# A radial network computed per edge block, dense products two node groups later, and own rows summed last, in a three-stage graph kernel

## The reference, cut to what matters

```python
# stage A and B: two preln GCN layers, N = 6250 nodes, D = 512, E = 100000 edges sorted by dst
h = layer_norm(x, g0, be0)                        # x is itself relu(layer_norm(input)) here
h = relu(gcn_conv(h, row, col, W0, b0) + h @ lw0.T + lb0); x_final = h
h = layer_norm(h, g1, be1)
h = relu(gcn_conv(h, row, col, W1, b1) + h @ lw1.T + lb1)
out = (x_final + h) @ pw.T + pb                   # row/col hold the edges and a loop per node
# stage C: equivariant messages; the radial network needs only the edges' 8 features
h = edge_feats                                    # (100000, 8)
for W in (W_mlp1, W_mlp2, W_mlp3):                # hidden 64
    h = SILU_2MOM * silu(h @ W / sqrt(W.shape[0]))
tpw = h @ W_mlp4 / sqrt(64)                       # weights of the messages, summed by receiver
```

## Time and profile before

| | us |
|---|---|
| median of 3 runs | 5891.26 |
| lowest and highest | 5843.2, 5891.44 |
| the profiled execution, its own time | 5896.5 |
| its span, first to last instruction | 5894.7 |
| layer 0, from its first own-row matmul to its last group's yb | 532.5 to 1809 |
| layer 1, the same | 1842 to 3392 |

### The profile page before, as it was taken

One profiled execution on the slowest core, in us unless ns is written; L12 is line 12 of the kernel. 1 busy time (PEld: TensorE's weight loads), 2 busy tenths in 40 slices (PEclk: granted clock), 3 DMA queues, 4 the chain that ended last, 5 costly groups with the idle time before them and its releaser, 6 DMA issues.

```text
span 5894.7 us, 104811 instructions
## 1 busy us (share of the span) xinstructions
PE 4878.7 (83%) x17136; PEld 2263.9 (38%) x17137; DVE 2857.1 (48%) x8231; ACT 2308.6 (39%) x6178; POOL 2737.7 (46%) x3492
## 2 busy tenths in 40 slices
PE   6897566778886567787777889999999999999988
PEld 5443122333332123333333334444444444444444
DVE  7542122334442112222222257777777777777776
ACT  0441000111110012233333466666666666666665
POOL 0334766666664766654433234444443333333332
PEclk9998678889997678899899999999999999999999
DMA  2233666677775666776666534444444334333333
GB/s 81 96 107 125 185 187 205 210 219 232 230 233 153 183 201 207 227 234 200 198 186 182 176 115 120 117 116 116 119 118 119 115 115 118 115 116 115 117 115 97
DMA packets 433673, 916.80 MB, mean 156 GB/s; under 512 B 63094, under 2 KB 170870, under 8 KB 433511
## 3 DMA queue, kind: packets, MB, share of 16 engines
q0 software_dynamic: 195840, 641.89, 37.5%
q1 hardware_dynamic: 237798, 274.56, 14.2%
HBM read 787.79 MB, written 128.41 MB: 155 GB/s over the span
## 4 chain that ended last, share of the span: by engine, by line
PE 31%; issue 21%; DVE 10%; DMA 8%; ACT 8%; DVEq 7%; ACTq 5%; POOL 5%; POOLq 2%; another core or an unknown queue 2%; SPq 1%
PE bank L1220 7%; DMA ring<-tab_d,idx 6%; POOL ring L559 4%; PE bank L1269 3%; PE bank L1350 3%; PE bank L1191 3%; PE bank L1193 3%; DVEq L1078 3%; ACT hB L756 3%; ACT dense_w L767 3%; ACTq L753 2%; PE bank L1253 2%; DVE hA L1086 2%; DMA tw<-tab_d 2%
## 5 line engine op out<-in xcount | busy, mean ns | idle before, releaser
L559 POOL DMA_INDIRECT ring<-tab_d,idx x1568 | 1541.6, 983 | 909.4 <-issue 549.1
L1350 PE MATMUL bank<-dense_w,oh 128*128 128x512 f32 x3520 | 1619.8, 603 | 66.9 <-DVE dense_w L1095 66.4
L1220 PE MATMUL bank<-ring,ohp 128*128 x3904 | 1084.6, 439 | 422.2 <-POOLq L569 330.9
L525 POOL DMA_INDIRECT ring<-up_d,idx x880 | 880.4, 1000 | 498.4 <-POOL idx L521 348.6
L767 ACT ACTIVATE dense_w<-hA,hC 128x128 f32<-128x128 f32 x2640 | 820.2, 389 | 654.8 <-DVE hA L1086 600.1
L1350 PEld LDWEIGHTS bank<-dense_w,oh 128*128 128x128 f32 x3520 | 633.1, 190 | 858.8 <-issue 668.1
L1220 PEld LDWEIGHTS bank<-ring,ohp 128*128 x3904 | 421.1, 108 | 1065.7 <-issue 763.6
L983 DVE TENSOR_TENSOR ohp<-iota_w,dst_f 128x512 f32 x392 | 266.1, 691 | 703.5 <-PE bank L1220 513.6
L521 POOL COPY idx<-src_i 128x2 int32 x440 | 81.2, 185 | 1045.2 <-DVE dense_w L1095 964.2
L1340 PE MATMUL bank<-w,hC 64*128 64x256 f32 x3520 | 501.9, 403 | 31.4 <-issue 22.9
L1072 DVE SCALAR_TENSOR_TENSOR hA<-ring,hC,hB 128x128 f32<-128x128 f32 x880 | 270.4, 348 | 490.3 <-ACT hB L756 428.3
(11 more groups left out here) (180 smaller groups left out, 4877.2 us busy)
## 6 DMA issues: line engine op xcount, KB each, us to landing
hC<-hid_d SPq DMA_DIRECT2D x440, 64.0 KB
tab_d<-tout SPq DMA_DIRECT2D x98, 256.0 KB, 2.7
tw<-tab_d SPq DMA_DIRECT2D x98, 256.0 KB
hlw<-hl_d SPq DMA_DIRECT2D x98, 256.0 KB
ring<-tab_d,idx POOLq DMA_INDIRECT x1568
hid_d<-hC SPq DMA_DIRECT2D x98, 256.0 KB
hl_d<-agg SPq DMA_DIRECT2D x74, 256.0 KB, 3.0
ring<-up_d,idx POOLq DMA_INDIRECT x880
```

Source lines behind the costliest of these rows:

```text
L525: g_.indirect_dma_start(ring_v[:, b, k, :], None, table, bass.IndirectOffsetOnAxis(idx_t[:, b, k:k + 1], 0)).then_inc(S["got"][b], 16)
L559: g_.indirect_dma_start(ring_h[:, b, k, :], None, table, bass.IndirectOffsetOnAxis(idx_b[:, b, k:k + 1], 0)).then_inc(S["got"][b], 16)
L1220: ins = pe.matmul(bank[0][:, :], ohp_b[:, bass.ds(at, 1), k, :].rearrange("p b n -> p (b n)"), ring_b[:, bass.ds(slot, 1), k, h, :].rearra ...
L1350: ins = pe.matmul(bank[h][:, :], oh[:, b, k, :], msg[:, b, k, h, :], start=False, stop=False, skip_group_check=True)
```

## The change

- **Radial per block.** In layer 1, PE and ACT take a step of the radial network after each edge block's visit, one piece per step, in the first 94 blocks: PE layer3(n), layer2(n+1), layer1(n+2), ACT act3(n), act2(n+1), act1(n+2), store_hid(n), load_ef(n+3). The first pieces' steps run ahead of the layer, the last three pieces are finished after it. ACT, not SP, now issues the feature loads (in layer 1, and the first two ahead of layer 0) and the stores of hid. One bank for each layer (4, 5, 6).
- **Later dense work.** Layer 0's turn, copy_at and dense run with delay 2 instead of 1, high, low and the stores with 3; turn now stands ahead of edge_sum. In layer 1 turn_xs, copy_xT and project have delay 2, residual, std, relu_h and store_x1 3, turn_h, copy_hT, up, up_out and store_up 4; both transposes stand ahead of edge_sum. up has bank 7 to itself.
- **Own rows last.** edge_sum starts bank 0 with the first visited block (group 0: an empty matmul) and waits for tw only after the group's last visit; the two own-row matmuls end the sum. load_self waits for sum_done.
- **Gathers.** Copy of the next indices and row 2 come before the wait for the block before and "arrived".

```diff
@@ -388,7 +387,7 @@
         S = G[L]
         def load_self(w, S=S, L=L):
-            after(sp, S["self_used"], w)
+            after(sp, S["sum_done"], w)
             sp.dma_start(tw[:, :], rows(tab_d[L], w)).then_inc(S["self_in"], 16)
         def load_hl(w, S=S, L=L):
@@ -426,32 +425,18 @@
             sp.wait_ge(S["up_ready"], w + 1)
             sp.dma_start(rows(up_d, w), uo[:, :]).then_inc(S["up_stored"], 16)
...
         if L == 0:
-            peeled(sp, [(0, load_self), (0, load_hl), (1, store_r), (2, store_tab), (2, store_hl)])
+            peeled(sp, [(0, load_self), (0, load_hl), (1, store_r), (3, store_tab), (3, store_hl)])
             sp.wait_ge(S["r_stored"], 16 * NW)
             sp.wait_ge(S["tab_stored"], 16 * NW)
             sp.wait_ge(S["hl_stored"], 16 * NW)
         else:
-            peeled(sp, [(0, load_ef), (0, load_self), (3, store_up), (0, load_hl), (4, store_hid), (0, load_r0),
-                        (1, load_x), (2, store_x1)])
+            peeled(sp, [(0, load_self), (0, load_hl), (0, load_r0), (2, load_x), (3, store_x1), (4, store_up)])
             sp.wait_ge(S["x1_stored"], 16 * NW)
             sp.wait_ge(S["up_stored"], 16 * NW)
-    sp.wait_ge(hid_out[0], 16 * (NG // 8))
-    sp.wait_ge(hid_out[1], 16 * (NG // 8))
+    sp.wait_ge(hid_out, 16 * (NG // 4))
     c = sp.alloc_register("sp_tp_count")
     sp.reg_mov(c, 1)
@@ -564,11 +549,11 @@
                     g_.reg_add(d, d, 1)
                     row(0)
                     row(1)
+                    g_.tensor_copy(idx_b[:, (b + 1) % NK, :], src_i[:, bass.ds(ahead, BT)]).then_inc(S["idx_ready"], 1)
+                    row(2)
                     with g_.If(n > LAG):
                         g_.wait_ge(S["got"][(b - LAG) % NK], landed)
                         g_.nop().then_inc(S["arrived"], 1)
-                    g_.tensor_copy(idx_b[:, (b + 1) % NK, :], src_i[:, bass.ds(ahead, BT)]).then_inc(S["idx_ready"], 1)
-                    row(2)
                     row(3)
                     g_.reg_add(c, c, 1)
                 pick(g_, g_.snap(n % NK), 0, NK, gather)
@@ -702,42 +687,89 @@
         def up_out(w, S=S):
             ac.wait_ge(S["up_done"], w + 1)
             after(ac, S["up_stored"], w, 16)
-            ac.copy(uo[:, :], bank[3][:, :]).then_inc(S["up_ready"], 1)
...
+            ac.copy(uo[:, :], bank[7][:, :]).then_inc(S["up_ready"], 1)
+        def act1(i):
+            ac.wait_ge(m1, i + 1)
+            if not isinstance(i, int) or i > 0:
+                ac.wait_ge(m2, i)
+            ac.activation(hA[:, 0, :], bank[4][:, :], ACT.Silu).then_inc(a1, 1)
+        def act2(i):
+            ac.wait_ge(m2, i + 1)
+            if not isinstance(i, int) or i > 0:
+                ac.wait_ge(m3, i)
+            ac.activation(hB[:, 0, :], bank[5][:, :], ACT.Silu).then_inc(a2, 1)
+        def act3(i):
+            ac.wait_ge(m3, i + 1)
+            to = hC[:, i % 2, :] if isinstance(i, int) else hC[:, bass.ds(i % 2, 1), :].rearrange("p b n -> p (b n)")
+            ac.activation(to, bank[6][:, :], ACT.Silu).then_inc(a3, 1)
+        def load_ef(i):
+            if not isinstance(i, int) or i > 1:
+                ac.wait_ge(ef_in, i * 16)
+                ac.wait_ge(m1, i - 1)
+            to = ef[:, i % 2, :] if isinstance(i, int) else ef[:, bass.ds(i % 2, 1), :].rearrange("p b n -> p (b n)")
+            ac.dma_start(to, a["ef_t"][:, bass.ds(i * D, D)]).then_inc(ef_in, 16)
+        def store_hid(i):
+            ac.wait_ge(a3, i + 1)
+            if not isinstance(i, int) or i > 0:
+                ac.wait_ge(hid_out, i * 16)
+            of = hC[:, i % 2, :] if isinstance(i, int) else hC[:, bass.ds(i % 2, 1), :].rearrange("p b n -> p (b n)")
+            ac.dma_start(hid_d[bass.ds(i * 4, 4), :, :].rearrange("g p e -> p g e"),
+                         of.rearrange("p (g e) -> p g e", g=4)).then_inc(hid_out, 16)
+        if L == 1:
+            c = ac.alloc_register("act_radial_count")
+            ac.reg_mov(c, 1)
+            def radial(w, c=c):
+                lo, hi = block_range(ac, w)
+                with ac.Fori(lo, hi) as g:
+                    n = ac.snap(c)
+                    with ac.If(n < NG // 4 - 3):
+                        act3(n)
+                        act2(n + 1)
+                        act1(n + 2)
+                        store_hid(n)
+                        load_ef(n + 3)
+                    ac.reg_add(c, c, 1)
         if L == 0:
-            peeled(ac, [(1, relu_r), (2, high), (1, std), (1, scaled), (1, copy_at)])
+            load_ef(0)
+            load_ef(1)
+            peeled(ac, [(1, relu_r), (3, high), (2, copy_at), (1, std), (1, scaled)])
         else:
-            peeled(ac, [(1, act1), (1, relu_r), (2, std), (2, relu_h), (2, act2), (1, copy_xT), (3, act3),
-                        (2, copy_hT), (2, up_out), (4, lambda w: None)])
+            act1(0)
+            load_ef(2)
+            act2(0)
+            act1(1)
+            load_ef(3)
+            act3(0)
+            act2(1)
+            act1(2)
+            store_hid(0)
+            peeled(ac, [(1, relu_r), (2, copy_xT), (4, copy_hT), (0, radial), (3, std), (3, relu_h), (4, up_out)])
+            last = NG // 4 - 1
+            act3(last - 2)
+            act2(last - 1)
+            act1(last)
+            store_hid(last - 2)
+            act3(last - 1)
+            act2(last)
+            store_hid(last - 1)
+            act3(last)
+            store_hid(last)
     c = ac.alloc_register("act_tp_count")
     ac.reg_mov(c, 1)
-    for b in range(2):
-        ac.wait_ge(hid_out[b], 16 * (NG // 8))
+    ac.wait_ge(hid_out, 16 * (NG // 4))
     ac.nop().then_inc(M["w13"], 1)
     ac.nop().then_inc(M["p2"], 1)
     lo_r, hi_r = ac.alloc_register("act_tp_lo"), ac.alloc_register("act_tp_hi")
@@ -1046,9 +1078,9 @@
             scale(0).then_inc(S["scale"], 1)
         if L == 0:
-            peeled(ve, [(1, layer_out), (0, onehots), (2, low), (1, second_norm)])
+            peeled(ve, [(1, layer_out), (0, onehots), (3, low), (1, second_norm)])
         else:
-            peeled(ve, [(1, layer_out), (0, onehots), (1, project_in), (2, residual)])
+            peeled(ve, [(1, layer_out), (0, onehots), (1, project_in), (3, residual)])
     c = ve.alloc_register("dve_tp_count")
@@ -1206,21 +1238,36 @@
         pe.reg_mov(v_r, 1)
         pe.nop().then_inc(S["used"], NV)
-        def edge_sum(w, S=S, c=c, v_r=v_r):
+        def layer1(i):
+            pe.wait_ge(ef_in, (max(i, 1) + 1) * 16 if isinstance(i, int) else i * 16 + 16)
+            if not isinstance(i, int) or i > 0:
+                pe.wait_ge(a1, i)
+            at = ef[:, i % 2, :] if isinstance(i, int) else ef[:, bass.ds(i % 2, 1), :].rearrange("p b n -> p (b n)")
+            pe.matmul(bank[4][:, :], w1[:, :], at, start=True, stop=True).then_inc(m1, 1)
+        def layer2(i):
+            pe.wait_ge(a1, i + 1)
+            if not isinstance(i, int) or i > 0:
+                pe.wait_ge(a2, i)
+            pe.matmul(bank[5][:, :], w2[:, :], hA[:, 0, :], start=True, stop=True).then_inc(m2, 1)
+        def layer3(i):
+            pe.wait_ge(a2, i + 1)
+            if not isinstance(i, int) or i > 0:
+                pe.wait_ge(a3, i)
+            pe.matmul(bank[6][:, :], w3[:, :], hB[:, 0, :], start=True, stop=True).then_inc(m3, 1)
+        def edge_sum(w, S=S, L=L, c=c, v_r=v_r):
             lo, hi = block_range(pe, w)
             after(pe, S["y_read"], w)
-            pe.wait_ge(S["self_in"], (w + 1) * 16)
-            pe.matmul(bank[0][:, :], ident_h[:, :], tw[:, 0:D], start=True, stop=False, skip_group_check=True)
-            pe.matmul(bank[0][:, :], ident_h[:, :], tw[:, D:], start=False, stop=False,
-                      skip_group_check=True).then_inc(S["self_used"], 1)
-            def visit(slot, at):
+            def visit(slot, at, first):
                 for k in range(BT):
                     for h in range(2):
                         ins = pe.matmul(bank[0][:, :],
                                         ohp_b[:, bass.ds(at, 1), k, :].rearrange("p b n -> p (b n)"),
                                         ring_b[:, bass.ds(slot, 1), k, h, :].rearrange("p b n -> p (b n)"),
-                                        start=False, stop=False, skip_group_check=True)
+                                        start=(first and k == 0 and h == 0), stop=False, skip_group_check=True)
                 ins.then_inc(S["used"], 1)
                 pe.reg_add(v_r, v_r, 1)
@@ -1228,15 +1275,25 @@
                 v, n = pe.snap(v_r), pe.snap(c)
                 slot, at = pe.snap((n - 1) % NK), pe.snap(v % NV)
                 pe.wait_ge(S["onehot"], v)
-                visit(slot, at)
+                visit(slot, at, True)
+            else:
+                touch(bank[0][:, :], D, True)
             with pe.Fori(lo, hi) as g:
                 v, n = pe.snap(v_r), pe.snap(c)
                 slot, at = pe.snap(n % NK), pe.snap(v % NV)
```

(35 more changed lines are left out.)

56 lines of the change are left out of this document (2 added, 54 removed).

## The result

The changed kernel takes 5673.23 us (median of 4 runs, 5664.33 to 5696.5) beside 5891.35 for the kernel before: a ratio of 0.9653, 95% interval 0.9594 to 0.9712. It is 3.5% faster; the forecast was 5460 us, 7.3%. The profiled execution has a span of 5662.4 us, 232 less than the one before.

A forecast was written before the change was run, and what follows sets the result against it. POOL's gathers were taken to pace early groups, PE and its order the late ones. Stage savings of 437 us, 299 of them in late layer 1, came off 5896.5 us to give 5460, range 5370 to 5600.

The forecast's parts named there:

- (a): Gather block on POOL: with the landing wait behind row 2, 5.4 us a block instead of 5.8, bounds 5.1 and 5.8.
- rival B: Gather blocks: the landing wait only moves, blocks stay at 5.8 to 6.1 us; total 5590 us, chance 0.14.
- (b): Layer 0, dense work later: a late group costs PE 8.3 us plus 1.73 per visit; late window 335 us, -34.
- (c): Early layer 1, radial per block: added work hidden behind POOL; -10 us in group 0, -26 in groups 1 to 11.
- Rival D: Early layer 1: the radial loop between PE and ACT serialises on hid stores; 11 us a block, 5985 us, chance 0.03.
- (d): Late layer 1 without radial work: POOL becomes the bound, 624 us instead of 923, -299.
- rival A: DMA crowds: the engines deliver no more than a share of 0.8 over a stretch; total 5536 us, chance 0.25.
- Rival C: Late layer 1: the group chain stays the limit through ACT's order and load_self; 740 us, total 5576, chance 0.13.
- (e): Bank and semaphore changes and the Ifs at 0; tail of layer 1 at 0, bounds -10 and +10; stage three untouched.

The follow-up runs named there:

- e3: Changed kernel with the old order of the gather block: 0.9871 of the kernel before.
- e12: Changed kernel with the old gather order and the feature load first in ACT's radial step: 0.978 of the kernel before.
- e13: Changed kernel with the old gather order, a repeat of e3 on another chip: 0.9859 of the kernel before.
- e17: Changed kernel with the old gather order, a repeat of e3 on a third chip: 0.9871 of the kernel before.
- e18: Changed kernel with the old gather order and the feature load first, a repeat of e12 on another chip: 0.9789 of the kernel before.
- e14: Kernel before with the new gather order alone, a repeat of e4 on another chip: 0.9821 of the kernel before.
- e4: Kernel before with the new gather order alone: 0.982 of the kernel before.
- e1: Changed kernel with the feature load first in ACT's radial step, ahead of activations and hid store: 0.9491 of the kernel before.
- e2: Changed kernel with the feature load ahead of the hid store but still behind act1: 0.9548 of the kernel before.
- e15: Changed kernel with the feature load first, a repeat of e1 on another chip: 0.9497 of the kernel before.
- e16: Changed kernel unchanged, timed on a chip where the kernel before takes 5796 us: 0.9677 of the kernel before.
- e11: Changed kernel unchanged, on a chip where the kernel before takes 5932 us: 0.9616 of the kernel before.
- e9: Changed kernel with the feature load first, the same as e1, on the chip of e11: 0.9561 of the kernel before.
- e7: e1 with the last three radial steps finished inside the loop instead of after layer 1: 0.9581 of the kernel before.
- e10: Kernel before with the new gather order alone, the same as e4, on the chip of e11: 1.0139 of the kernel before.

## Why the prediction was wrong

(a) Gather block: right in size, on the 5800 kind. Group 0 there is (159.4 - 2)/30 = 5.2 us a block (5.4 taken, 5.1 the floor), groups 1 to 12 took 424 (420 forecast). On the first chip they took 176 and 442.5, which is 34 of layer 0's missing 59 us; with them go the holes of long instructions in the loop itself, a cost that no row of before showed. The landing wait was not the limit there, as argued: POOL waits 1.5 us for landings in all of group 0. So rival B's mechanism is out, though group 0's (176 - 2)/30 = 5.8 us a block on the first chip is B's number.

(b) Late layer 0: PE's side was right. From the changed kernel's PE timeline, one group of three visits:

```profile
1731.32 0.60 PE L1302 MATMUL bank<-ident,t 128*128 128x128 f32 x4
1731.76 5.34 PE L1267 MATMUL bank<-ring,ohp 128*128 x24
...
1737.37 3.60 PE L1310 MATMUL bank<-dense_w,AT 128*128 128x512 f32 x8
1740.80 3.60 PE L1312 MATMUL bank<-dense_w,AT 128*128 128x512 f32 x8
1744.23 0.60 PE L1302 MATMUL bank<-ident,t 128*128 128x128 f32 x4
```

It takes 12.9 us, 8.3 + 3×1.73 = 13.5 was the sum, and none of the earlier trace rows's three waits is left. PE is busy for 322.08 us of the window, the very number forecast, but the window is 354 and not 335: 32 us of waiting and not 13. On the 5800 kind it is 360 to 370 in the changed kernel with the old order (e3, e12, e13, e17, e18), 357 and 364 with the new order alone (e14, e4), and 347 to 353 with both (e1, e2, e15, e16). So the later dense work, 27 us by rival B's count, brings some 10 beside the new order. PE's waits in this window say why, two rows of e14, then the one row of e16:

```profile
PE bank L1253 <- ACT AT L679: 15.5, 23, 0.7
PE bank L1245 <- DVE t L1019: 13.4, 15, 0.9
...
PE bank L1267 <- POOLq L556: 32.0, 15, 4.4
```

The 29 us of waits for the dense operands went, as forecast, and PE waits 32 us for gathers to arrive in their place, while POOL waits 10.8 us for PE: the two hold each other up in turn, POOL more than PE, which costs more than the 13 us added for it.

(c) Early layer 1: the step that failed. "Its waits, for the previous store and load, reach back a block" holds for the store: in the first result's profile and in e16 ACT never waits for one, and with the load first 16 of the 94 wait, 21 us in all (e15). It does not hold for the load. The load is issued at the end of ACT's step and needed by layer1 of PE's next step. Its landing takes 3.5 us, and from layer1's start back to the next load's issue it is 2.1 (medians of e16): 5.6 us with nothing else in the way, more than the 5.4 of a block, and 6.1 as measured. I had counted what the step costs ACT in issue time and PE in matmuls (both right: with the load first, on the 5800 kind, the windows are 174 and 426 for 167 and 425), but not closed the ring from a load's issue over its landing, layer1, act1 and the store's issue back to the next load. Rival D had the mechanism, PE and ACT taking turns over a DMA inside the loop, with the wrong transfer and the wrong size: 91 us over 94 blocks is 1.0 us a block on the 5800 kind, where D needed 4.6 to decide the sign. On the 5900 kind, the first result's, the same edit takes groups 0 to 11 from 735.5 us (e11) to 695.2 (e9), with 592 forecast: 40 us there are shown to be the load's, and the 103 that stay go with the long instructions. That last is read from profiles beside each other, not from an edit, so of the first chip's 130 us in early layer 1 the part beyond the load stays open in its cause.

(d) Late layer 1: right, in the time (624 forecast, 625 measured, 625 to 658 over the ten profiles of the changed code with the new order) and in the place: POOL paces it. The DMA share is 0.77, not 0.85, so the transfer times behind rival A were 10% too long. Rival C (740) is out.

(e) Nothing for the Ifs: no run tried them by themselves. The tail came to +0.9, within its bounds, of which e7 shows 10 us to be the late radial steps. Stage three was not touched, yet it is 2464.9 to 2475.1 us in all fifteen profiles of kernels with the changed code and 2455.1 to 2458.8 in the five with the code of before, whatever the order of gathers. I had it at 0; its 16 us are open, and no run tried them.

So the term mis-sized most is (c): +94 for -36. With the load moved and no long instructions, e15's 5504 us are 44 from the forecast's 5460. Its ratio is 0.950 and not the forecast 0.927 because the kernel before, too, is some 90 us quicker on the 5800 kind; it was not profiled there, so in which stages stays open.

## What to carry to other kernels

When work is moved into a software-pipelined loop, follow each DMA from its issue to its landing to its first reader and back to its next issue, and sum that ring; a load at the end of an in-order engine's step adds all that stands ahead of it in the step to its ring, while at the head of the step it costs the same and does not. Where two limits sit on one loop, an edit tried alone understates its worth (45 to 51 and 103 us for the same line here). And time a change of a few per cent on more than one chip: one order of four instructions read 0.982 and 1.014.

## What was not expected of the hardware

A 32 KB load by ACT's queue takes 1.8 to 6.6 us from issue to landing, 3.5 in the median (e16; 3.0 in e2, where it goes out ahead of the 256 KB store). The Trainium skill ("DMA: Bandwidth & Descriptors", Anatomy of one DMA) gives 2.0 us plus bytes/436e3 for the software path, an estimate of 2.1 us for this size; the ring's 5.6 us would then be 1.4 shorter, 4.2, and the load would not have bound. The measurement, on a hardware queue with full gather traffic beside it, decides.

Chips, or groups of runs on them, differ by more than the runs of one group do: the kernel before takes 5796 to 5803 us on three chips and 5891 to 5932 on the first and two others, and the kernel with the gather order alone 5693 (e14) and 6016 (e10). The second has 469 register and branch instructions of 0.6 to 0.8 us from 530 to 3140 us, the first has none over 0.24.
